# Four changes at once to a one-core transformer block: residual buffers, a load's queue, paired score products and the routing test

## The chip, the cores and the metric

The kernel runs on one core of a Trainium2 chip. The core has five engines with an instruction stream each: TensorE (PE, matrix products into PSUM), VectorE (DVE), ScalarE (ACT), GpSimd (POOL) and SyncE (SP), which here only issues transfers. The engines wait for each other through semaphores. The metric is the device time of one execution in microseconds; lower is better.

## The reference

Input and output are 8 x 1024 rows of 256 numbers, in float32. The block has three parts, each added to its input:

```python
x = x + 0.5 * ffn(layernorm(x))
x = x + attention(layernorm(x))
x = x + 0.5 * ffn(layernorm(x))
```

`attention` is causal, with 16 heads of 16 numbers, a relative position bias from a table, and an output projection `y @ W_proj.T + b_proj`. `ffn` is larger than its name:

```python
y1 = ln(x + mha(x))                 # 4 heads of 64, over the 8 rows of axis 0
gates = softmax(xf @ wg)            # 8 experts
idx = argmax(gates)
mask1 = one_hot(idx, E)
loc = sum((cumsum(mask1, 0) - 1) * mask1, -1)   # place in the expert's line
keep = loc < cap                    # cap = 8192 / 8 = 1024
slot = where(keep, idx * cap + loc, E * cap)
h = einsum('ecd,edf->ecf', disp, w1) + b1       # disp: the kept rows by slot
y = einsum('ecf,efd->ecd', h, w2) + b2
out = where(keep, gate_val * y[slot], 0)
return ln(y1 + out)
```

There is no nonlinearity between the expert's two products, so the kernel multiplies its weights w1 and w2 first and applies one 256 x 256 matrix to each row.

## The kernel before

The rows are cut into 64 tiles of 128 (`TILES`), and four tiles make a group, of which there are 16 (`NG`). The program is fully unrolled: `each(count, body)` calls `body(n, n % 2)`. A stage is a `Phase` with one block of code for each engine, and the order on each engine is the order in which the code is written. A semaphore count that an engine waits for is the only tie between them. The stages are: constants; the first FFN (attention, routing, gather and expert products); the projection to queries, keys and values; the attention core; the output projection; the second FFN in the same code as the first.

**Output projection** (`attention_out`). Per group POOL copies the attention's result into `y` (L2314), PE transposes it (8 records, L2330), ACT and DVE copy the transposed tiles out (L2356, L2374), and PE makes 16 records of products in two halves (L2346). DVE adds the projection's bias to the residual that SP has loaded into `xr` (L2382) and then the product of each half (L2387, twice). ACT's queue stores `xr` (L2364). `xr` has two buffers, and the load of group n waits for the store of group n - 2 (L2304 issues the load).

**Attention core** (`attention_core`). A unit is four heads of one sequence. SP loads for each unit the queries (twelve transfers, L1829), the keys (six, L1833), the transposed near bias `biasT` (eight, L1838) and the near bias (L1847), in this order. PE's first products (L1906) want keys and queries, DVE's first instruction (L2197) the near bias, ACT's first (L2098) `biasT`.

**FFN attention** (`ffn_attention`). PE's order is written out by hand, and a tile's scores (L439) are four products, one for each head: queries of the head pair `qT[:, u, h // 2]` stationary, keys `kT[:, u, h]` moving, 128 columns. `kT` is zero where the other head of the pair lies, so both heads of a pair have the same stationary side. L428 is the product to the values, of 256 columns.

**Routing** (`ffn`). `link` makes DVE wait for its own instruction before the next one. After `attend_vector`, the half's attention code, DVE makes the mask, the places, the slots and the free slots that dropped rows go to, and then eight chunks of one-hot tiles with which PE builds the inverse list (L1269). The part of a chunk that holds the gate values is scaled by ACT (L1132), and for the chunks in `MINE` by DVE (L1420). A dropped row of rank r gets the offset of the interval of free slots [fbeg, fend) in which r lies: `a3` is (r >= fbeg), `b3` is (r < fend) (L1388), their product (L1389) times `off` (L1390) is summed over the experts.

## Time and profile before

| | us |
|---|---|
| Runs of the kernel before | 2779.59, 2789.35, 2786.78 (median 2786.78) |
| Profiled execution, its own time | 2785.7 |
| Its span in the profile | 2784.0 |
| PE busy | 2344.2 (84%) |
| DVE busy | 2148.9 (77%) |
| ACT busy | 1658.3 (60%) |
| POOL busy | 838.5 (30%) |
| FFN attention, first and second half | 19 to 487, 2059 to 2522 |
| Routing, first and second | 487 to 538, 2522 to 2574 |
| Gather and expert products | 538 to 760, 2574 to 2784 |
| Attention core | 981 to 1967 |
| Output projection | 1967 to 2059 |

The stages' bounds are read from the timeline. A row of the trace names the line of the kernel, the engine, the operation, what it writes and reads, its shape and how often it stands there. A time in brackets is how long the engine sat idle before it, and what ended that. "PEld" is the loading of a product's stationary side, which runs beside PE's products. "SPq" and "ACTq" are the transfers that an engine issues.

### The profile page before, as it was taken

What the parts mean: (1) busy time and instruction counts of PE and PEld (TensorE: products, weight loads), DVE (VectorE), ACT (ScalarE), POOL (GpSimd) and SP (SyncE); (2) the same over time, 40 slices, a digit from 0 to 9 for tenths busy, and PEclk for the clock granted to TensorE, in tenths of its full rate; (3) what the DMA queues carried; (4) which work ended last, traced back from release to release, by engine and by line L of the source; (5) the groups of instructions that cost most, each with busy time, mean ns of one, the idle gap of its engine ahead of it and who ended that gap; (6) DMA issues with size and microseconds to landing.
All of it is one profiled execution on the core that took longest, in us unless ns stands there. A gap on an engine that the chain in (4) does not pass through costs nothing. (4 is left out here: it accounts for less than half of the span.)

```text
span 2784.0 us, 46914 instructions
## 1 busy us (share of the span) xinstructions
PE 2344.2 (84%) x15864; PEld 1420.1 (51%) x15864; DVE 2148.9 (77%) x5653; ACT 1658.3 (60%) x3995; POOL 838.5 (30%) x853
## 2 busy tenths in 40 slices
PE   5999998867479959999999999999869999994263
PEld 4666665745345514444444444444646666663243
DVE  5888887727779868889898898987447888877067
ACT  3455453416534439999999999999315455452154
POOL 2343443264634420000000000000123343431746
PEclk8999999879789969999999999999989999996677
DMA  4132214372245464454554554542441121211722
GB/s 121 52 100 72 69 51 140 131 254 102 79 138 169 160 129 98 95 108 99 102 105 94 107 105 93 110 99 45 131 149 54 46 69 46 69 46 46 207 80 76
DMA packets 244687, 281.60 MB, mean 101 GB/s; under 512 B 41808, under 2 KB 212880, under 8 KB 243808
## 3 DMA queue, kind: packets, MB, share of 16 engines
q1 hardware_dynamic: 218192, 218.81, 30.7%
q0 software_dynamic: 16384, 50.35, 5.7%
q10 hardware_dynamic: 9872, 9.45, 1.0%
q8 instruction: 127, 2.08, 0.3%
q14 instruction: 112, 0.92, 0.1%
HBM read 190.63 MB, written 94.16 MB: 102 GB/s over the span
## 5 line engine op out<-in xcount | busy, mean ns | idle before, releaser
L2197 DVE CUSTOM_DVE_ANT_0 banks<-banks,attn_bias 128x128 f32<-128x128 f32 (+7 forms) x1024 | 760.1, 779 | 109.3 <-PE banks L1906 83.2
L2110 ACT ACTIVATE attn_probT<-banks 128x512 f32<-128x512 f32 x1152 | 623.6, 623 | 61.3 <-PE banks L1923 50.7
L1906 PE MATMUL banks<-attn_kst,attn_qst 96*128 96x512 bf16 (+3 forms) x1536 | 421.3, 336 | 23.1 <-DMA attn_kst<-kparts 13.0
L1923 PE MATMUL banks<-attn_qst,attn_kst 99*128 99x256 bf16 (+3 forms) x2176 | 411.6, 281 | 14.7 <-ACT attn_probT L2110 7.1
L1945 PE MATMUL banks<-attn_probT,attn_vb 128*32 128x256 f32 (+3 forms) x4352 | 316.2, 400 | 7.8 <-ACT attn_probT L2110 7.4
L1923 PEld LDWEIGHTS banks<-attn_qst,attn_kst 99*128 99x128 bf16 x2176 | 187.2, 97 | 169.6 <-ACT attn_probT L2110 55.5
L2255 POOL CAST attn_lowp<-attn_lowT 128x32 bf16<-128x32 f32 x64 | 13.5, 211 | 851.3 <-DVE attn_lowT L2205 851.3
L410 PE MATMUL banks<-ffn_xT,winT 128*128 128x512 f32 x512 | 250.9, 613 | 6.0 <-ACT ffn_w L610 2.9
L1906 PEld LDWEIGHTS banks<-attn_kst,attn_qst 96*128 96x128 bf16 x1536 | 117.4, 97 | 256.0 <-DVE attn_low L2197 158.5
L2098 ACT COPY banks<-attn_biasT 128x512 f32<-128x512 f32 x384 | 228.4, 630 | 28.5 <-DMA attn_biasT<-neardT 21.8
L870 POOL TENSOR_TENSOR ffn_xs<-ffn_xs,row_ffn_out 128x1024 f32<-128x1024 f32 x32 | 75.4, 2356 | 416.3 <-DVE ffn_xs L752 390.2
L580 ACT ACTIVATE ffn_xs<-banks,ffn_xs 128x128 f32<-128x128 f32 x512 | 182.9, 380 | 13.1 <-DVE ffn_xs L717 11.5
L1945 PEld LDWEIGHTS banks<-attn_probT,attn_vb 128*32 128x32 f32 x4352 | 106.4, 109 | 133.4 <-ACT attn_probT L2110 70.0
L619 ACT COPY ffn_xs<-banks 128x256 f32<-128x256 f32 x128 | 48.3, 377 | 203.5 <-PE banks L459 200.2
L1083 POOL DMA_INDIRECT ffn_xs<-rows,ffn_inv x128 | 123.1, 962 | 148.5 <-DVE ffn_inv L1424 94.5
L1318 PE MATMUL banks<-ffn_w,ffn_xT 128*128 128x256 f32 x512 | 130.4, 408 | 44.0 <-issue 31.4
L610 ACT ACTIVATE ffn_w<-banks,ffn_qk_b 64x512 f32<-64x512 f32 x128 | 87.4, 683 | 128.0 <-PE banks L410 127.2
L717 DVE TENSOR_REDUCE ffn_xs<-banks 128x4 f32<-128x512 f32 x128 | 88.5, 692 | 92.3 <-PE banks L439 92.1
L439 PEld LDWEIGHTS banks<-ffn_w,ffn_xs 128*128 128x128 f32 x1024 | 135.6, 200 | 23.7 <-issue 20.3
L439 PE MATMUL banks<-ffn_w,ffn_xs 128*128 128x128 f32 x1024 | 145.3, 287 | 0.8 <-DVE ffn_xs L739 0.8
L2197 DVE DVE_READ_ACCUMULATOR2_ANT attn_low<- 128x1 f32 x1024 | 144.9, 141 | 0.1
L725 DVE TENSOR_SCALAR ffn_xs<-ffn_xs 128x128 f32<-128x128 f32 x512 | 137.5, 331 | 4.5
(254 smaller groups left out, 4500.2 us busy)
## 6 DMA issues: line engine op xcount, KB each, us to landing
rows<-ffn_xs SPq DMA_DIRECT2D x64, 512.0 KB, 3.1
attn_qst<-qparts SPq DMA_DIRECT2D x384, 64.0 KB, 2.8
attn_kst<-kparts SPq DMA_DIRECT2D x192, 128.0 KB, 4.9
ffn_xs<-in_L_ffn_w_dram SPq DMA_DIRECT2D x16, 1024.0 KB
attn_biasT<-neardT SPq DMA_DIRECT2D x128, 128.0 KB, 4.9
attn_bias<-neard SPq DMA_DIRECT2D x128, 128.0 KB, 2.2
qparts<-qkv_part SPq DMA_DIRECT2D x32, 384.0 KB, 2.8
kparts<-qkv_part SPq DMA_DIRECT2D x32, 384.0 KB, 2.8
```

The source lines that it names most:

```text
L410: mm = nc.tensor.matmul(bank[QK], core.winT[:, k, j * P:(j + 1) * P], xT[:, u, k, :], start=(k == 0), stop=(k == KB - 1))
L439: mm = nc.tensor.matmul(bank[SC[t % 2]][:, h * P:(h + 1) * P], qT[:, u, h // 2, t * P:(t + 1) * P], kT[:, u, h, t * P:(t + 1) * P], start= ...
L580: ins = nc.scalar.activation(prob[:, t % 2, h, :], bank[SC[t % 2]][:, h * P:(h + 1) * P], ACT.Exp, bias=negm[:, t % 2, h:h + 1], scale=1.0 ...
L725: ins = nc.vector.tensor_scalar(prob[:, t % 2, h, :], prob[:, t % 2, h, :], rinv[:, t % 2, h:h + 1], None, ALU.mult)
L1083: pool.indirect_dma_start(xs[:, n, t, :], None, rows, bass.IndirectOffsetOnAxis(ap=inv[:, i:i + 1], axis=0)).then_inc(s_got[n % 2], 16)
L1318: mm = nc.tensor.matmul(part, xT[:, u, k, t * P:(t + 1) * P], w12[:, k, expert(n, u)], start=False, stop=(k == KB - 1), skip_group_check=True)
L1906: mm = nc.tensor.matmul(score[k % 2][:, a:e], qst[0:K6, u, half, hh, ii * P:(ii + 1) * P], kst[0:K6, u, hh, a:e], start=True, stop=True)
L1923: mm = nc.tensor.matmul(tbank[t % 3][:, at:at + nb * P], kst[:, u, hh, j * P:(j + 1) * P], qst[:, u, half, hh, x:x + nb * P], start=(k == ...
L1945: mm = nc.tensor.matmul(obank[32 * hh:32 * hh + 32, x:x + nb * P], vb[:, u, j, hh, :], probT[:, g % 2, i, at:at + nb * P], start=hh not in ...
L2098: nc.scalar.copy(tbank[t % 3].rearrange("p (a c) -> p a c", a=2), over(near[:, 0:2 * P], 2, 1)).then_inc(s_seed, 1)
L2110: nc.scalar.activation(probT[:, g % 2, i, 0:w], tbank[t % 3][:, 0:w], ACT.Exp, scale=-1.0).then_inc(s_exp, 1)
L2197: nc.vector.tensor_tensor_reduce(out=part, in0=part, in1=bias[:, hh, T - w:T], scale=1.0, scalar=BIG, op0=ALU.add, op1=ALU.min, accum_out= ...
```

## The change

Four places are edited. (1) In the output projection `xr` gets four buffers (`XR = 4`), each with its own load and store semaphores, so the load of group n waits for the store of group n - 4. (2) In the attention core the six key loads of the first unit are issued by ACT, ahead of all its work, and no longer by SP; those of later units stay on SP. (3) In FFN attention one product makes two heads' scores: the moving side is 256 columns, two products a tile. (4) In routing the interval test becomes a sum of steps: with `step` the difference of neighbouring offsets, the sum over e of (r >= fbeg[e]) * step[e] is the offset of the last interval that begins at or below r. Two 512-column operations go and two small ones come. Five small operations move from the routing chain to the start of the FFN phase, and `MINE` is (3, 7) in place of (2, 5).

```diff
@@ -435,10 +435,10 @@
...
             if not (under(n, 1) and t < 2):
                 pe.wait_ge(s_seed, 4 * n + t - 1)
-            for h in range(FH):
-                mm = nc.tensor.matmul(bank[SC[t % 2]][:, h * P:(h + 1) * P], qT[:, u, h // 2, t * P:(t + 1) * P],
-                                      kT[:, u, h, t * P:(t + 1) * P], start=False, stop=(h == FH - 1),
-                                      skip_group_check=True)
+            for j in range(FH // 2):
+                mm = nc.tensor.matmul(bank[SC[t % 2]][:, 2 * j * P:(2 * j + 2) * P].rearrange("p (h c) -> p h c", h=2),
+                                      qT[:, u, j, t * P:(t + 1) * P], kT[:, u, 2 * j:2 * j + 2, t * P:(t + 1) * P],
+                                      start=False, stop=(j == FH // 2 - 1), skip_group_check=True)
             mm.then_inc(s_sps, 1)
 
...
@@ -936,7 +936,7 @@
...
     FB = FF // P
     CT = TILES // NG * 2
-    MINE = (2, 5)
+    MINE = (3, 7)
     with Phase(core, name) as ph:
         logits = ph.sb("logits", [P, TILES, NE])
...
@@ -957,12 +957,12 @@
...
         onb, ona = lent(0, CHUNKS, CT, P), lent(4, CHUNKS, CT, 2 * TILES)
         dif, ex, cand = (lent(8 + i / 4, TILES, NE) for i in range(3))
-        hot, scan, a3, b3 = (lent(9 + i / 4, NE, TILES) for i in range(4))
+        hot, scan, a3 = (lent(9 + i / 4, NE, TILES) for i in range(3))
         w1 = [lent(10 + i, KB, FF) for i in range(2)]
         w2 = [lent(12 + i, FB, C) for i in range(4)]
         onest = tile("onest", TILES)
-        eidx, ebase, tot, cnt, free, fend, fbeg, off = (tile(n, NE) for n in (
-            "eidx", "ebase", "tot", "cnt", "free", "fend", "fbeg", "off"))
+        eidx, ebase, tot, cnt, free, fend, fbeg, off, step = (tile(n, NE) for n in (
+            "eidx", "ebase", "tot", "cnt", "free", "fend", "fbeg", "off", "step"))
         ei = tile("ei", NE, dt=I32)
         rowtot = tile("rowtot", NE + 1)
...
@@ -1337,16 +1337,19 @@
...
                 dve.wait_ge(s_dve, n[0])
 
-            attend_vector(dve)
-            over_yet(dve)
             V = nc.vector
-            link(V.tensor_reduce(mx[:, :], logits[:, :, :], AX.X, ALU.max))
-            V.tensor_tensor(dif[:, :, :], logits[:, :, :], over(mx[:, :], NE, 2), ALU.subtract).then_inc(s_dif, 1)
             dve.wait_ge(s_iota, 1)
             link(V.tensor_copy(eidx[:, :], ei[:, :]))
             link(V.tensor_scalar(ebase[:, :], eidx[:, :], float(CAP), None, ALU.mult))
             link(V.memset(onest[:, :], 1.0))
-
+            dve.wait_ge(s_ib, 1)
+            link(V.tensor_copy(ib_f[:, :], ib[:, :]))
+            dve.wait_ge(s_ni, 1)
+            link(V.tensor_copy(number[:, :], ni[:, :]))
+            attend_vector(dve)
+            over_yet(dve)
+            link(V.tensor_reduce(mx[:, :], logits[:, :, :], AX.X, ALU.max))
+            V.tensor_tensor(dif[:, :, :], logits[:, :, :], over(mx[:, :], NE, 2), ALU.subtract).then_inc(s_dif, 1)
             dve.wait_ge(s_dif, 1)
             link(V.tensor_scalar(cand[:, :, :], dif[:, :, :], 0.0, -float(NE), ALU.is_ge, ALU.mult))
...
@@ -1376,6 +1379,8 @@
...
             link(V.tensor_tensor(off[:, :], ebase[:, :], cnt[:, :], ALU.add))
             link(V.tensor_tensor(off[:, :], off[:, :], fbeg[:, :], ALU.subtract))
+            V.tensor_copy(step[:, 0:1], off[:, 0:1])
+            link(V.tensor_tensor(step[:, 1:NE], off[:, 1:NE], off[:, 0:NE - 1], ALU.subtract))
 
             dve.wait_ge(s_ex, 1)
...
@@ -1385,9 +1390,7 @@
...
             link(V.tensor_scalar(rank[:, :], dscan[:, :], base[:, NE:NE + 1], -1.0, ALU.add, ALU.add))
             link(V.tensor_tensor(a3[:, :, :], over(rank[:, :], NE, 1), over(fbeg[:, :], TILES, 2), ALU.is_ge))
-            link(V.tensor_tensor(b3[:, :, :], over(rank[:, :], NE, 1), over(fend[:, :], TILES, 2), ALU.is_lt))
-            link(V.tensor_tensor(a3[:, :, :], a3[:, :, :], b3[:, :, :], ALU.mult))
-            link(V.tensor_tensor(a3[:, :, :], a3[:, :, :], over(off[:, :], TILES, 2), ALU.mult))
+            link(V.tensor_tensor(a3[:, :, :], a3[:, :, :], over(step[:, :], TILES, 2), ALU.mult))
             link(V.tensor_reduce(t2[:, :], a3[:, :, :].rearrange("p e t -> p t e"), AX.X, ALU.add))
             link(V.tensor_tensor(t2[:, :], t2[:, :], rank[:, :], ALU.add))
...
@@ -1400,10 +1403,6 @@
...
             link(V.tensor_copy(bf[:, :], bcol[:, :]))
             link(V.tensor_copy(af[:, :], acol[:, :]))
-            dve.wait_ge(s_ib, 1)
-            link(V.tensor_copy(ib_f[:, :], ib[:, :]))
-            dve.wait_ge(s_ni, 1)
-            link(V.tensor_copy(number[:, :], ni[:, :]))
             for u in range(2):
                 stored(dve, u)
...
@@ -1817,6 +1816,12 @@
...
             return isinstance(n, int) and n == NU - 1
 
+        def load_keys(queue, n, u):
+            for r, a in enumerate(K_PARTS):
+                queue.dma_start(kst[r * AD:(r + 1) * AD, u, :, :],
+                                kd[bass.ds(n * HG * AD, HG * AD), a, :].rearrange("(h d) t -> d h t", d=AD)
+                                ).then_inc(s_load[u], 16)
+
         block = ph.block()
 
...
@@ -1829,10 +1834,8 @@
...
                                      qd[bass.ds(n * HG * AD, HG * AD), a, half * HW:(half + 1) * HW].rearrange(
                                          "(h d) t -> d h t", d=AD)).then_inc(s_load[u], 16)
-                for r, a in enumerate(K_PARTS):
-                    sp.dma_start(kst[r * AD:(r + 1) * AD, u, :, :],
-                                 kd[bass.ds(n * HG * AD, HG * AD), a, :].rearrange("(h d) t -> d h t", d=AD)
-                                 ).then_inc(s_load[u], 16)
+                if not under(n, 1):
+                    load_keys(sp, n, u)
                 for hh in range(HG):
                     for at, w in ((0, 2 * P), (2 * P, P)):
...
@@ -2087,6 +2090,8 @@
...
         @block.scalar
         def _(act):
+            load_keys(act, 0, 0)
+
             def seed(n, u, t):
                 pieces = TILE[t][4]
...
@@ -2284,13 +2289,14 @@
...
 
     nc = core.nc
+    XR = 4
     rows, outs = (a.rearrange("(g t p) c -> g p t c", p=P, t=GT) for a in (x, out))
     with Phase(core, "proj") as ph:
         y = ph.sb("y", [P, 2, GT, C])
         yT = ph.sb("yT", [P, 2, KB, GW])
-        xr = ph.sb("xr", [P, 2, GT, C])
-        s_load = [ph.sem("load0"), ph.sem("load1")]
-        s_store = [ph.sem("store0"), ph.sem("store1")]
+        xr = ph.sb("xr", [P, XR, GT, C])
+        s_load = [ph.sem(f"load{i}") for i in range(XR)]
+        s_store = [ph.sem(f"store{i}") for i in range(XR)]
         s_y, s_xb, s_tps, s_tsb0, s_tsb1, s_ops, s_osb = (ph.sem(x) for x in (
             "y", "xb", "tps", "tsb0", "tsb1", "ops", "osb"))
...
@@ -2299,10 +2305,11 @@
...
         def _(sp):
             def body(n, u):
-                if not under(n, 2):
-                    sp.wait_ge(s_store[u], (n - u) * 8)
-                sp.dma_start(xr[:, u, :, :], rows[bass.ds(n, 1), :, :, :].rearrange(
-                    "o p t c -> p (o t) c")).then_inc(s_load[u], 16)
+                v, turns = n % XR, n // XR
+                if turns:
+                    sp.wait_ge(s_store[v], 16 * turns)
+                sp.dma_start(xr[:, v, :, :], rows[bass.ds(n, 1), :, :, :].rearrange(
+                    "o p t c -> p (o t) c")).then_inc(s_load[v], 16)
             each(NG, body)
 
...
@@ -2362,10 +2369,10 @@
...
                 act.wait_ge(s_osb, 2 * n + 2)
                 act.dma_start(outs[bass.ds(n, 1), :, :, :].rearrange("o p t c -> p (o t) c"),
-                              xr[:, u, :, :]).then_inc(s_store[u], 16)
+                              xr[:, n % XR, :, :]).then_inc(s_store[n % XR], 16)
             each(NG, body)
-            for u in range(2):
-                act.wait_ge(s_store[u], 16 * (NG // 2))
+            for v in range(XR):
+                act.wait_ge(s_store[v], 16 * (NG // XR))
 
         @block.vector
...
@@ -2378,15 +2385,16 @@
...
                 if not (isinstance(n, int) and n == NG - 1):
                     yT_out(n + 1, 1 - u)
-                dve.wait_ge(s_load[u], (n - u) * 8 + 16)
-                nc.vector.tensor_tensor(xr[:, u, :, :], xr[:, u, :, :], over(core.rows["proj"][:, :], GT, 1),
+                v = n % XR
+                dve.wait_ge(s_load[v], 16 * (n // XR + 1))
+                nc.vector.tensor_tensor(xr[:, v, :, :], xr[:, v, :, :], over(core.rows["proj"][:, :], GT, 1),
                                         ALU.add).then_inc(s_xb, 1)
                 dve.wait_ge(s_xb, n + 1)
                 for h in range(2):
                     dve.wait_ge(s_ops, 2 * n + h + 1)
-                    nc.vector.tensor_tensor(xr[:, u, 2 * h:2 * h + 2, :],
+                    nc.vector.tensor_tensor(xr[:, v, 2 * h:2 * h + 2, :],
                                             bank[4 + h].rearrange("p (t c) -> p t c", t=2),
-                                            xr[:, u, 2 * h:2 * h + 2, :], ALU.add).then_inc(s_osb, 1)
+                                            xr[:, v, 2 * h:2 * h + 2, :], ALU.add).then_inc(s_osb, 1)
             each(NG, body)
 
...
```

How the instructions move is seen in the order on three engines. On PE, in the first FFN's attention, a stretch before and in the change (`ffn_w` and `ffn_xs` are the memory that `qT` and `kT` lie in):

```order
 L410 MATMUL banks<-ffn_xT,winT 128x512 x6
 L393 MATMUL banks<-ident,ffn_xs 128x128 x4
-L439 MATMUL banks<-ffn_w,ffn_xs 128x128 x8
-L393 MATMUL banks<-ident,ffn_xs 128x128 x4
-L428 MATMUL banks<-winT,ffn_xT 128x256 x4
-L439 MATMUL banks<-ffn_w,ffn_xs 128x128 x4
...
+L439 MATMUL banks<-ffn_w,ffn_xs 128x256 x4
+L393 MATMUL banks<-ident,ffn_xs 128x128 x4
+L428 MATMUL banks<-winT,ffn_xT 128x256 x4
+L439 MATMUL banks<-ffn_w,ffn_xs 128x256 x2
```

The four products of a tile have become two of twice the width, at the same place between the same neighbours. In the trace each of these float32 products is two records, so a tile has eight records of 128 columns before.

On SP, at the start of the attention core, before:

```order
L1829 DMA attn_qst<-qparts 16x4x512 x12
L1833 DMA attn_kst<-kparts 16x4x1024 x6
L1838 DMA attn_biasT<-neardT 128x256
...
L1847 DMA attn_bias<-neard 128x256 x4
L1829 DMA attn_qst<-qparts 16x4x512 x12
```

and the same place in the change, where L1834 is the query load, L1841 `biasT`, L1850 the near bias and L1821 the keys of the second unit:

```order
L1834 DMA attn_qst<-qparts 16x4x512 x12
L1841 DMA attn_biasT<-neardT 128x256
...
L1850 DMA attn_bias<-neard 128x256 x4
L1834 DMA attn_qst<-qparts 16x4x512 x12
L1821 DMA attn_kst<-kparts 16x4x1024 x6
```

The first unit's keys are gone from between the queries and the tables; they stand at the head of ACT's stream, before its first copy from `biasT`.

On DVE, at the start of each FFN phase (here the first):

```order
 L159 UNCONDITIONAL_BRANCH
 L1331 UNCONDITIONAL_BRANCH
+L1342 CAST ffn_eidx<-ffn_ei 128x8
+L1343 TENSOR_SCALAR ffn_ebase<-ffn_eidx 128x8
+L1344 MEMSET ffn_onest 128x64
+L1346 CAST ffn_ibf<-ffn_ib 128x128
+L1348 CAST ffn_number<-ffn_ni 128x64
 L791 MEMSET ffn_w 128x4096
 L767 MEMSET gatew 128x128
```

Five small operations, which stood in the routing chain as L1346 to L1348, L1404 and L1406, stand ahead of the memset that opens the phase.

## Rows read from the trace of the kernel before

**Rows 1.** Groups by line, 1960 to 2059 (busy us, mean ns, idle before).

```profile
L2346 PE MATMUL banks<-wprojT,proj_yT 128*128 128x256 f32 x256 | 60.4, 390 | 11.3 <-DVE proj_xr L2387 11.3
...
L2382 DVE TENSOR_TENSOR proj_xr<-proj_xr,row_proj 128x1024 f32<-128x1024 f32 x16 | 20.5, 1282 | 31.8 <-DMA proj_xr<-x 31.8
```

**Rows 2.** Waits of SP's queue, 1965 to 2062 (total us, times, longest).

```profile
SPq L2304 <- DMA x<-proj_xr: 75.9, 14, 9.5
```

**Rows 3.** Timeline of the output projection (start, us, instruction, idle before).

```profile
1974.82 3.62 PE L2346 MATMUL banks<-wprojT,proj_yT 128*128 128x256 f32 x16
...
1978.47 0.69 DVE L2387 TENSOR_TENSOR proj_xr<-banks,proj_xr 128x512 f32<-128x512 f32 x1 [0.59 <-PE banks L2346]
...
1979.15 3.62 PE L2346 MATMUL banks<-wprojT,proj_yT 128*128 128x256 f32 x16
...
2049.80 3.69 PE L2346 MATMUL banks<-wprojT,proj_yT 128*128 128x256 f32 x16 [1.61 <-DVE proj_xr L2387]
...
2054.37 1.29 DVE L2387 TENSOR_TENSOR proj_xr<-banks,proj_xr 128x512 f32<-128x512 f32 x2
```

**Rows 4.** Windows (engines' busy us, PEclk, DMA share, GB/s).

```profile
1990.00:2010.00 20.00, 17.39 (x94) 14.75 (x92) 9.52 (x13) 2.35 (x4) 3.43 (x4) 1.00 0.63 202
995.00:1000.00 5.00, 1.58 (x5) 0.45 (x5) 1.54 (x7) 2.23 (x4) 0.01 (x1) 0.50 1.14 286
```

**Rows 5.** DMA issues, 1950 to 2060 (KB each, us to landing).

```profile
proj_xr<-x SPq DMA_DIRECT2D x16, 512.0 KB, 3.9
```

**Rows 6.** Timeline at the start of the attention core.

```profile
987.17 2.77 SPq L1833 DMA_DIRECT2D attn_kst<-kparts  x6
...
993.77 1.85 SPq L1847 DMA_DIRECT2D attn_bias<-neard  x4
...
995.43 0.48 PE L1906 MATMUL banks<-attn_kst,attn_qst 96*128 96x128 bf16 x2 [12.98 <-DMA attn_kst<-kparts]
...
998.25 0.30 DVE L2197 CUSTOM_DVE_ANT_0 banks<-banks,attn_bias 128x128 f32<-128x128 f32 x1 [13.87 <-DMA attn_bias<-neard]
```

**Rows 7.** Timeline of the second routing.

```profile
2524.18 2.67 POOL L863 TENSOR_TENSOR ffn_xs<-ffn_xs,row_ln_b 128x1024 f32<-128x1024 f32 x1
2524.57 2.31 DVE L1346 CAST ffn_eidx<-ffn_ei 128x8 f32<-128x8 int32 x1
...
2541.10 0.69 DVE L1388 TENSOR_TENSOR ffn_xs<-ffn_rank,ffn_fend 128x512 f32<-128x512 f32 x1
...
2546.77 0.23 DVE L1404 CAST ffn_ibf<-ffn_ib 128x128 f32<-128x128 int32 x1
```

**Rows 8.** Timeline at the end of the second routing.

```profile
2568.12 2.02 PE L1269 MATMUL banks<-ffn_xs 128*128 128x128 f32 x16 [1.28 <-ACT ffn_xs L1132]
...
2570.77 2.02 PE L1269 MATMUL banks<-ffn_xs 128*128 128x128 f32 x16 [0.63 <-ACT ffn_xs L1132]
```

**Rows 9.** Timeline where the two FFN halves start.

```profile
23.59 2.34 POOL L877 TENSOR_TENSOR ffn_xs<-ffn_xs,row_ln_b 128x1024 f32<-128x1024 f32 x1 [3.67 <-DMA ffn_xs<-in_L_attn_x_dram]
...
23.88 2.08 DVE L769 TENSOR_TENSOR fourth<-ident 128x16 f32<-128x16 f32 x1
...
2060.01 3.47 DVE L791 MEMSET ffn_w<- 128x4096 f32 x1 [4.35 <-PEq L2288]
...
2063.39 1.34 DVE L677 BATCH_NORM_STATS2 ffn_xs<-ffn_xs 128x6 f32<-128x256 f32 x4
```

**Rows 10.** Timeline: scores beside another product, and a slowed score block.

```profile
2134.01 1.92 PE L439 MATMUL banks<-ffn_w,ffn_xs 128*128 128x128 f32 x8
...
2192.70 1.89 PE L428 MATMUL banks<-winT,ffn_xT 128*128 128x256 f32 x8
...
2194.42 1.05 PE L439 MATMUL banks<-ffn_w,ffn_xs 128*128 128x128 f32 x8
...
2195.32 0.60 PE L449 MATMUL banks<-ident,ffn_xs 128*128 128x128 f32 x4
```

**Rows 11.** Timeline during the second gather.

```profile
2623.09 1.97 PE L1223 MATMUL banks<-ident,ffn_y 128*128 128x128 f32 x8 [23.40 <-issue]
```

## The prediction

> **What bounds the kernel now.** The page's busy shares come first: PE is busy 84% of the span, DVE 77%, ACT 60%, so no stage is short of work and each edit has to be read in its own stage. Then the trace, stage by stage.
>
> In the output projection (1967 to 2059) the groups by line show PE's product L2346 idle for 11.3 us on DVE's additions, and DVE's L2382 idle for 31.8 us on the load of the residual [rows 1]. SP's queue, which issues that load, stands for 75.9 us in 14 waits for the store out of the same buffer [rows 2]. Sixteen groups go through two buffers, so 14 loads wait for a store: this stage is bound by the round "add, store, load, add", not by an engine. The timeline shows the pace without the wait: the second and third product begin at 1974.82 and 1979.15, 4.33 us apart, while the last begins at 2049.80 [rows 3], which is (2049.80 - 1979.15)/13 = 5.43 us a group on average.
>
> At the start of the attention core nothing but transfers goes on. SP issues the six key loads from 987.17 for 2.77 us, then the tables, the last of them from 993.77; PE begins at 995.43 with the keys, DVE at 998.25 with the near bias [rows 6].
>
> In routing DVE runs one chain, each instruction waiting for the last, and PE and ACT follow; in FFN attention PE is nearly always busy, and the scores are a part of its own row of work.
>
> **Output projection, two more buffers.** What a buffer's turn must hold can be read off the pace. L2382 starts about 0.8 us after its group's product and the second L2387 ends 4.34 us after it (1978.47 + 0.69 - 1974.82 [rows 3]), so at 5.43 us a group two buffers leave 2 x 5.43 - 3.54 = 7.3 us for the store and the load after it; that is just what the pair takes, which agrees with a landing of 3.9 us for a load [rows 5] and about as much for a store. Four buffers at 4.33 us leave 4 x 4.33 - 3.54 = 13.8 us. The pair could take almost twice its time before DVE waits again. So I expect SP's waits to end unnoticed and every group at 4.33. What is late next is PE itself: 16 products and 8 transposes fill the 4.33 (3.62 of it in L2346 [rows 3]), and DVE has about 3.2 us of work in a group. The last product then begins at 1974.82 + 13 x 4.33 + 3.46 = 2034.57 (the last group has no transposes ahead of it: 16 records at 0.2155 us), the last addition ends 4.34 later at 2038.91, and before it ended at 2054.37 + 1.29 = 2055.66 [rows 3]. That is **-16.7 us**. Nothing excludes a part of it: the 1.05 MB of a group in 4.33 us is 242 GB/s, and this stage moved 202 GB/s [rows 4]. That the engines can carry more is seen at the start of the core, with 286 GB/s [rows 4]. I take -16.7; the bounds are 0 and -16.8.
>
> **Core start, keys on ACT's queue.** SP's table loads move forward by the 2.77 us that the keys' six issues took [rows 6]. ACT has nothing to do then: its first work waits for biasT, issued after the keys. The order on ACT is six issues and then that work, so nothing is held up. DVE's start at 998.25 is the end of a load issued from 993.77, 4.5 us before, so it can come to about 995.5, and PE's 995.43 goes earlier too. The other end is 0: in 995 to 1000 the transfers filled the DMA engines (share 1.14 [rows 4]), so earlier issue may only mean a longer queue. Bounds -2.8 and 0; I take the issue, since DVE's start lies 4.5 us behind the first issue of its load, close to the 3.9 us that a load takes elsewhere [rows 5]. **-2.5 us**.
>
> **Routing.** Gone from the chain of the second half: L1388 and its product L1389, 0.73 us each from start to start (0.69 long [rows 7]), against two step operations of 1 and 7 columns, which I put at 0.14 each (an estimate: less than the 0.23 of L1404): -1.17. The moved L1404 and its like L1406 took from 2546.77 to 2547.26: -0.49 [rows 7]. The other three moved ones look dearer than they are. L1346 took 2.31 us for 8 columns, and it ends at 2526.88, when POOL's L863 does (2524.18 + 2.67 = 2526.85) [rows 7]: it was held by POOL, and the next instruction on DVE, the 512-column L1351, is of the kind that I expect to be held in its place. So I take from these three only what lay behind POOL's end, about 0.45 us, where the upper end is 2.31 and some 0.4 for the two short ones, 2.7.
>
> The Trainium skill bears on this (SBUF — State Buffer, section "SBUF: two separate sides"): DVE and GpSimd share a port pair as an exclusive lock, and the loser stands for the whole instruction. The row agrees to 0.03 us. By that rule the gain is the 0.45, without it 2.7.
>
> At the end of routing PE waits for ACT's scaling before each of its last two blocks, 0.63 us each, and starts them 2.65 us apart [rows 8]; 16 records at 0.1115 are 1.78. With chunk 7 scaled on DVE the last one follows at once: -0.86. Together -3.0 in the second half. The five moved operations stand there at the head of DVE's line, ahead of the memset L791 that starts at 2060.01 and directly behind which L677 begins the chain of the half [rows 9]: five of them at L1404's 0.23 or a little less, +1.1. Net **-1.9 us**. In the first half DVE has slack at the start: L769 took 2.08 us for 16 columns, again held by POOL [rows 9], so the 1.1 disappears; without that cover it would cost 1.1. At the end of that routing ACT, busy with weight copies, sets the time, so the shorter DVE chain brings nothing and only the last block counts: **-0.9 us** (range 0 to -3).
>
> **Scores.** A tile's scores are 8 records of 128 columns at 0.1115 us each, 0.89 us; the block of L439 starts 0.90 us before what follows it. L428 runs 8 records of 256 columns in 2194.42 - 2192.70 = 1.72 us [rows 10], so four take 0.86. The stationary side is loaded half as often, but these loads lie beside matmuls now. So 0.03 us a tile; 64 tiles in each of two halves stand on PE's own line: 128 x 0.03 = **-3.5 us**. Other blocks of L439 take 0.99 from start to start; if two heads a product removed the 0.1 as well, it is 128 x 0.11 = -14. The low end is -3 or, were the two-head form to read its operand slower, 0. I take the small value, since the 0.1 stands at a block's edge, which stays.
>
> **Clock.** In 8 of 28 iterations of FFN attention the granted clock fell and a score block took 1.92 us in place of 1.05 (eight rows like the one at 2134.01 [rows 10]), with some 1.55 us lost in the iteration. The blocks are rearranged in time, so this number can be 3 or 14 after: -8 to +9 us, taken as 0.
>
> **Sum.** -16.7 - 2.5 - 1.9 - 0.9 - 3.5 = -25.5. The profiled execution took 2785.7 us (span 2784.0); the median of the runs, 2786.8, is 1.1 above. 2785.7 - 25.5 = 2760.2, and on the median's footing 2761.
>
> **The rivals.**
> *The forecast*, four buffers free the projection and the small ones add: 2761. Chance 0.77.
> *Transfers hold the projection.* If 202 GB/s were the limit, 1.05 MB takes 5.2 us, a gain of 14 x 0.26 = 3.6 in place of 16.7: 2761 + 13 = 2774. For it: the rate would have to rise by a fifth, with reads and writes mixed. Against it: the 286 GB/s, and that SP idled 75.9 us, so the present rate is made by the wait. Chance 0.11, half of it still faster by over 0.3%.
> *Scores save the block's edge too*: -14 in place of -3.5, 2750. Chance 0.07.
> *Slower: a longer starvation in the gather.* In the second FFN's expert stage PE stood 23.40 us with nothing to wait for that the profile shows [rows 11], while GpSimd gathered rows by DMA; it is likely the loading of PE's instructions behind those transfers. The change takes 1,024 records off PE ahead of it, so the point in the code at which this happens can shift. One more such stand in each half: +46.8, 2761 + 46.8 = 2808. It decides from 25.5 + 8.4 = 34 us, so one alone (2784) is no change. Against it: the stages behind attention are the same, instruction for instruction. Chance 0.05.
>
> The Trainium skill says of this (Runtime: NRT & Kernel Launch, section "Instruction fetch mechanics") that the engine fetches ahead in 16 KiB blocks and the cost is mostly hidden. By that rule this rival is nothing; the row of 23.40 us speaks against it.
>
> **How the numbers follow.** What a measurement can tell from no change is 0.3%, 8.4 us: from 2778.4 to 2795.2. Low end: scores at -14 and two or three dips fewer give 2746, so 2745. High end: the transfer-bound projection, 2774, and a few us of spread in the runs (2779.6 to 2789.4 before), 2777. Faster takes the forecast, the scores and half of the transfer case, 0.77 + 0.07 + 0.05 = 0.89, less 0.01 for mishaps; same is the rest of the transfer case and a single stand, 0.07; slower 0.05.
>
> **What would show it.** In the profile after: no or short waits of L2382 for its load, L2346 groups 4.33 apart, the stage some 17 us shorter; DVE's first L2197 some 2.5 us nearer to the start of the core; the 512-column instruction after the routing's subtraction taking about 2.3 in place of 0.43; L439 with 512 records of 256 columns at 0.2155. I am wrong if L2382's wait goes over to the load's landing (DMA share near full and groups over 5 us), if the gather's stands grow, or if L439's block costs over 0.9.

## The result and the profile after

The changed kernel takes 2763.36 us (median of four runs, 2759.59 to 2764.06), the kernel before 2786.66 (four runs). The ratio is 0.9912, 95% interval 0.9900 to 0.9924: 23.3 us faster, where 25.5 were forecast, inside the range of 2745 to 2777. The profiled execution of the changed kernel is its shortest run, 2759.59 us.

The head of its page (span; busy us, share, instructions):

```profile
span 2757.9 us, 45893 instructions
...
PE 2334.6 (85%) x15352; PEld 1387.7 (50%) x15352; DVE 2151.4 (78%) x5653; ACT 1657.1 (60%) x3995; POOL 838.6 (30%) x853
```

PE has 512 product records fewer and 9.6 us less of busy time. Each stage begins at an instruction that both traces have, so their stages can be laid side by side ("memset" is DVE's L791, which opens an FFN):

| stage (us) | before | after | difference | forecast |
|---|---|---|---|---|
| Constants | 19.43 | 20.66 | +1.2 | 0 |
| FFN 1, start to memset | 0.92 | 2.15 | +1.2 | hidden |
| FFN 1, attention | 466.73 | 465.29 | -1.4 | -1.75 |
| FFN 1, routing | 50.64 | 49.97 | -0.7 | -0.9 |
| FFN 1, gather and experts | 230.39 | 225.62 | -4.8 | 0 |
| Projection to queries, keys, values | 212.86 | 212.34 | -0.5 | 0 |
| Core, SP's first load to DVE's first L2197 (L2202 after) | 17.28 | 16.65 | -0.6 | -2.5 |
| Core, the rest | 969.11 | 968.24 | -0.9 | 0 |
| Output projection | 91.74 | 76.12 | -15.6 | -16.7 |
| FFN 2, start to memset | 0.91 | 2.15 | +1.2 | +1.1 |
| FFN 2, attention | 462.23 | 459.50 | -2.7 | -1.75 |
| FFN 2, routing | 50.59 | 47.32 | -3.3 | -3.0 |
| FFN 2, gather and experts | 211.17 | 211.89 | +0.7 | 0 |

**Output projection.** The groups by line, which answer to [rows 1] (product and bias addition are now L2353 and L2390):

```profile
L2353 PE MATMUL banks<-wprojT,proj_yT 128*128 128x256 f32 x256 | 57.7, 379 | 0.0
...
L2390 DVE TENSOR_TENSOR proj_xr<-proj_xr,row_proj 128x1024 f32<-128x1024 f32 x16 | 23.6, 1474 | 0.0
```

Both idle times have gone from 11.3 and 31.8 us to 0.0. SP's queue, the line that answers to [rows 2], still waits, 55.8 us in 12 waits where it was 75.9 us in 14, and the longest is the same:

```profile
SPq L2311 <- DMA x<-proj_xr: 55.8, 12, 9.5
```

This wait is now harmless: the loads run ahead of their use, so SP waits early for a buffer that nobody misses yet, and DVE's L2390 never stands for its load. The engine that uses the data has to be read, not the queue. The timeline (compare [rows 3]):

```profile
1962.01 3.31 PE L2337 MATMUL banks<-ident,proj_y 128*128 128x128 f32 x16 [2.13 <-POOL proj_y L2321]
...
1965.15 3.62 PE L2353 MATMUL banks<-wprojT,proj_yT 128*128 128x256 f32 x16
...
1969.48 3.62 PE L2353 MATMUL banks<-wprojT,proj_yT 128*128 128x256 f32 x16
...
2025.76 7.07 PE L2353 MATMUL banks<-wprojT,proj_yT 128*128 128x256 f32 x32
...
2032.87 0.69 DVE L2395 TENSOR_TENSOR proj_xr<-banks,proj_xr 128x512 f32<-128x512 f32 x1 [0.91 <-PE banks L2353]
```

The products stand 4.33 us apart (1969.48 - 1965.15), and from 1965.15 to 2025.76 there are 14 such steps, 60.61 us: none is stretched. The missing 1.1 us lies ahead of them. PE's first two sets of transposes took 3.31 us for 16 records, where they took 2.08 before. The granted clock fell to 0.50, the lower of its two levels (1.2 GHz), while PE stood idle for 2.13 us ahead of them, and rose to 1.00 (2.4 GHz) at 1964.8, while PE was busy. In the kernel before, PE came out of the same wait (2.14 us) at a granted clock of 1.00. So this is not of the change: among the profiles of the experiments the fall at the stage's start comes and goes, and E7, with the same four buffers at a clock of 1.00, takes 75.01 us for the stage.

**Core start**, to be held against [rows 6]:

```profile
976.04 2.75 ACTq L1821 DMA_DIRECT2D attn_kst<-kparts  x6
...
985.81 2.28 SPq L1850 DMA_DIRECT2D attn_bias<-neard  x4
...
989.86 0.48 PE L1909 MATMUL banks<-attn_kst,attn_qst 96*128 96x128 bf16 x2 [12.35 <-DMA attn_qst<-qparts]
...
992.68 0.30 DVE L2202 CUSTOM_DVE_ANT_0 banks<-banks,attn_bias 128x128 f32<-128x128 f32 x1 [13.24 <-DMA attn_bias<-neard]
```

The keys are issued at the stage's start by ACT, and the last table 9.78 us after it (985.81 - 976.03), where it was 12.80. But DVE starts 6.87 us behind that issue, where it was 4.48. Of the 3.0 us saved in issuing 2.4 went into the time from issue to DVE's start.

**Routing.** The 512-column instruction behind the second routing's subtraction (compare [rows 7]):

```profile
2500.61 2.67 POOL L863 TENSOR_TENSOR ffn_xs<-ffn_xs,row_ln_b 128x1024 f32<-128x1024 f32 x1
...
2501.12 2.45 DVE L1354 TENSOR_SCALAR ffn_xs<-ffn_xs 128x512 f32<-128x512 f32 x1
```

It ends 0.29 us behind GpSimd's instruction and takes 2.45 us, where the same operation stood at 0.43 before: it took the place of the 8-column one, as forecast. The end of the second routing, which answers to [rows 8]:

```profile
2539.51 2.02 PE L1269 MATMUL banks<-ffn_xs 128*128 128x128 f32 x16 [0.63 <-ACT ffn_xs L1132]
...
2542.16 3.81 PE L1269 MATMUL banks<-ffn_xs 128*128 128x128 f32 x32 [0.62 <-ACT ffn_xs L1132]
```

The last two blocks run as one piece of 32 records with one wait ahead of them. And the start of the second FFN (compare [rows 9]):

```profile
2037.20 0.18 DVE L1342 CAST ffn_eidx<-ffn_ei 128x8 f32<-128x8 int32 x1 [3.64 <-POOL ffn_ei L1072]
...
2038.08 0.20 DVE L1348 CAST ffn_number<-ffn_ni 128x64 f32<-128x64 int32 x1
2039.19 3.47 DVE L791 MEMSET ffn_w<- 128x4096 f32 x1 [0.92 <-DVE ffn_number L1348]
```

**Scores.** The score products in the groups by line:

```profile
L439 PE MATMUL banks<-ffn_w,ffn_xs 128*128 128x256 f32 x512 | 141.1, 400 | 0.8 <-DVE ffn_xs L739 0.8
```

512 records of 256 columns in place of 1,024 of 128. The starvation in the gather that a rival was built on, [rows 11], is still there, of the same length and at the same product:

```profile
2596.17 1.97 PE L1223 MATMUL banks<-ident,ffn_y 128*128 128x128 f32 x8 [23.40 <-issue]
```

### The profile page after: what moved, and what is told of

Its sections match the earlier page's. It is cut to its first block and busy times, and to the rows that moved or that the text cites. A ratio compares the mean times of both kernels' runs of the same rounds, so it can differ in the third digit from the quotient of the medians.

```text
span 2757.9 us, 45893 instructions
## 1 busy us (share of the span) xinstructions
PE 2334.6 (85%) x15352; PEld 1387.7 (50%) x15352; DVE 2151.4 (78%) x5653; ACT 1657.1 (60%) x3995; POOL 838.6 (30%) x853
## 5 line engine op out<-in xcount | busy, mean ns | idle before, releaser
L2202 DVE CUSTOM_DVE_ANT_0 banks<-banks,attn_bias 128x128 f32<-128x128 f32 (+7 forms) x1024 | 759.7, 778 | 108.1 <-PE banks L1909 82.8
L2260 POOL CAST attn_lowp<-attn_lowT 128x32 bf16<-128x32 f32 x64 | 13.4, 209 | 850.3 <-DVE attn_lowT L2210 850.3
L410 PE MATMUL banks<-ffn_xT,winT 128*128 128x512 f32 x512 | 250.7, 612 | 6.5 <-ACT ffn_w L610 2.9
L1318 PE MATMUL banks<-ffn_w,ffn_xT 128*128 128x256 f32 x512 | 130.3, 408 | 43.0 <-issue 30.7
L2202 DVE DVE_READ_ACCUMULATOR2_ANT attn_low<- 128x1 f32 x1024 | 143.8, 140 | 0.1
L439 PE MATMUL banks<-ffn_w,ffn_xs 128*128 128x256 f32 x512 | 141.1, 400 | 0.8 <-DVE ffn_xs L739 0.8
L410 PEld LDWEIGHTS banks<-ffn_xT,winT 128*128 128x128 f32 x512 | 90.3, 192 | 93.3 <-issue 73.8
```

Of the source, the lines that this page charges most:

```text
L410: mm = nc.tensor.matmul(bank[QK], core.winT[:, k, j * P:(j + 1) * P], xT[:, u, k, :], start=(k == 0), stop=(k == KB - 1))
L439: mm = nc.tensor.matmul(bank[SC[t % 2]][:, 2 * j * P:(2 * j + 2) * P].rearrange("p (h c) -> p h c", h=2), qT[:, u, j, t * P:(t + 1) * P], ...
L1318: mm = nc.tensor.matmul(part, xT[:, u, k, t * P:(t + 1) * P], w12[:, k, expert(n, u)], start=False, stop=(k == KB - 1), skip_group_check=True)
L2202: nc.vector.tensor_tensor_reduce(out=part, in0=part, in1=bias[:, hh, T - w:T], scale=1.0, scalar=BIG, op0=ALU.add, op1=ALU.min, accum_out= ...
```

## The experiments

They ran on two chips, E1 to E4 on the one that their results number 4 and E5 to E12 on number 8; the result of the first comparison names no chip. The kernel before takes 2716.57 us on chip 4 and 2715.1 to 2715.5 on chip 8, 70 less than in the first comparison (this is looked at in the last section). Each ratio is to runs of the kernel before on the same chip. The stages of the kernel before are from its own profile, E11, on chip 8. E3, E7, E8 and E9 ran once each and are read by their stages alone.

**E1, four buffers alone.** The edit to `attention_out` (`XR = 4` and its semaphores), nothing else.

> The kernel before with four residual buffers in the output projection and nothing else. Theory (the buffer round was the bound): the stage shortens by 15 to 16 us and the whole by the same, ratio about 0.9943; no wait of DVE's bias addition for its load. Rival (part of it is a phase between this stage and the others, or a given-back wait later): the stage shortens by 15 but the whole by less than 10.

2697.04 us against 2716.57, ratio 0.9927 (0.9910 to 0.9944): 19.5 us. The stage takes 76.45 us, 15.4 less than the 91.81 of E11. On E1's own chip the stage with two buffers takes 92.80 (E2), 95.54 (E3) and 92.94 us (E4). All four of these profiles have the fall of the clock at the stage's start, E3's the longest; against E2 and E4 the gain is 16.4 to 16.5. The buffer round is shown as the cause of the main gain; nothing was given back later. The interval of the whole, 15 to 24 us, holds all these figures.

**E5, three buffers.**

```diff
-    XR = 4
+    XR = 3
...
-                act.wait_ge(s_store[v], 16 * (NG // XR))
+                act.wait_ge(s_store[v], 16 * len(range(v, NG, XR)))
```

> The kernel before with three residual buffers. Theory (a buffer's round needs 7.3 us, three buffers at 4.33 us a group leave 9.45): the same gain as with four, 15 to 16 us in the stage. Rival (store and load take longer when they overlap more): only a part, 5 to 12 us, with waits of DVE's bias addition left.

2697.65 us, ratio 0.9935 (0.9919 to 0.9952), stage 74.93. Its groups by line:

```profile
L2348 PE MATMUL banks<-wprojT,proj_yT 128*128 128x256 f32 x256 | 57.8, 379 | 0.0
...
L2385 DVE TENSOR_TENSOR proj_xr<-proj_xr,row_proj 128x1024 f32<-128x1024 f32 x16 | 23.9, 1494 | 0.0
```

No idle time either. Three buffers do it, as the account of 9.45 against 7.3 us said; the fourth brings nothing measurable. The fair partner of this stage is E7's 75.01 with four buffers, since both have a granted clock of 1.00 at the stage's start; E12's 76.11 and E1's 76.45 have the fall.

**E2, the scores alone.**

> The kernel before with two heads per score product and nothing else. Theory (the saving of 0.12 us in an iteration of FFN attention is given back where DVE's L690 meets GpSimd's L858, which lasts 2.60 in place of 2.45 us): iterations of 26.72 and 26.87 us side by side, the whole unchanged within 2 us, ratio 0.999 to 1.001. Rival (as predicted, 0.03 us a tile): all iterations at 26.68, the whole 3.5 us shorter, ratio 0.9987. The number of clock dips may move it by 1.55 us each.

2714.9 us, ratio 0.9997 (0.9987 to 1.0007). The theory fell. It came from the trace of the changed kernel, in which iterations of 26.72 and 26.87 us (from one L495 to the next) alternate, where the kernel before has 26.80 only; the longer ones are those in which GpSimd's L858 lasts longer, with DVE's L690 held beside it. Both kinds in the changed kernel:

```profile
2107.86 2.45 POOL L858 TENSOR_TENSOR ffn_xs<-ffn_xs,row_ln_g 128x1024 f32<-128x1024 f32 x1 [1.72 <-DVE ffn_xs L711]
...
2134.57 2.60 POOL L858 TENSOR_TENSOR ffn_xs<-ffn_xs,row_ln_g 128x1024 f32<-128x1024 f32 x1 [1.73 <-DVE ffn_xs L711]
```

But E1, E3 and E4, which have the old scores, show 26.80 and 26.95 side by side, E5 and E11, with the old scores too, nearly only 26.80, and E12 and E7, with the new ones, only 26.72. So the 0.15 us of GpSimd comes with either kernel, and at each of its two levels the edit saves 0.08 us an iteration: 0.02 us a tile, not 0.03. The level goes with the chip more than with the edits: of the 32 instructions of L858 21 to 24 last 2.60 us or more in the four profiles of chip 4, and 0 to 4 in the eight of chip 8. Of four score blocks in an iteration three keep about 0.03 us each (0.96 from start to start in E12, 0.99 in E11); the first gives it up before PE's next product of L410 begins. For 128 tiles that is 2.6 us, which the interval of E2 (-3.5 to +1.9 us) neither excludes nor shows; the saving rests on the iterations.

**E3, the keys on ACT's queue alone.**

> The kernel before with the first unit's keys loaded from ACT's queue and nothing else. Theory (the transfers' bytes set the start): DVE's first instruction in the core comes 0.6 us nearer to the stage's start than in the kernel before (17.28 us). Rival (the issue sets it): 2.5 us nearer.

DVE starts 16.84 us after the stage's start, in E11 17.04. E1, E2, E4, E5 and E11, with the keys on SP, have 16.83 to 17.05; E3, E7, E8 and E12, with the keys on ACT, 16.13 to 16.84. The queue is worth 0 to 0.9 us, not 2.5.

**E6, near bias first.** In the changed kernel, for the first unit:

```diff
+                if under(n, 1):
+                    near(0)
                 for hh in range(HG):
                     for at, w in ((0, 2 * P), (2 * P, P)):
                         sp.dma_start(biasT[:, u, hh, at:at + w],
...
             load(0, 0)
-            near(0)
             load(1, 1)
```

> The changed kernel with the near bias of the first unit loaded before its transposed near bias. Theory (DVE's first instruction waits for the last of the first unit's bytes): DVE starts the core 1.5 to 3 us earlier, just behind PE's first product, and the whole gains that much, unless ACT, whose table now lands later, takes it back: then 0. Rival (all is landed at one time whatever the order): no change at all in DVE's start, 16.6 us from the stage's start.

**E9, the same with the keys back on SP.**

> The changed kernel with the near bias before its transposed form, and the first unit's keys back on SP's queue. Theory (what DVE's start waits for is the last byte ahead of it, so the order matters and the queue that issues hardly): DVE starts 14.3 to 14.6 us after the stage's start, against 14.0 with the keys on ACT, 16.6 to 16.9 with the near bias last. Rival (both edits are needed): 16 us or more.

E6: 13.99 us from the stage's start. E9: 14.61. Against the same queue in the old order (16.13 to 16.84, and 16.83 to 17.05) the order of the loads is worth 2.1 to 2.9 us at DVE's start; E6 against E9 gives the queue 0.6. Near bias and DVE's start in E9 and, below, in E10, which has E6's core:

```profile
957.41 1.85 SPq L1851 DMA_DIRECT2D attn_bias<-neard  x4
...
963.21 0.30 DVE L2200 CUSTOM_DVE_ANT_0 banks<-banks,attn_bias 128x128 f32<-128x128 f32 x1 [11.21 <-PE banks L1909]
```

```profile
952.41 1.85 SPq L1852 DMA_DIRECT2D attn_bias<-neard  x4
...
960.13 0.50 PE L1910 MATMUL banks<-attn_kst,attn_qst 96*128 96x128 bf16 x2 [11.95 <-POOL attn_kst L2275]
...
960.60 0.30 DVE L2203 CUSTOM_DVE_ANT_0 banks<-banks,attn_bias 128x128 f32<-128x128 f32 x1 [10.49 <-PE banks L1910]
```

DVE now waits for PE's first product and no longer for a load. In E10 the stage starts at 946.70, and PE waits for GpSimd's memset of the key rows, which ends 13.4 us after the stage's start in every profile, and not for a transfer. In E6 and E9 PE still waits for its transfers, and starts 0.1 and 0.7 us later than in E10. So memset and transfers are late next, close together. ACT, which waits for `biasT`, starts 1.6 us later than with the old order (E6 17.80 us from the stage's start, E8 16.19) and in E9 3.3 later (19.86, against 16.54 in E11), and that takes part of the gain back: from the stage's start to the output projection E6 takes 982.71 us, E10 983.44, E9 984.20, E12 984.43, E8 984.86, E11 986.04. E6 as a whole: 2690.82 us, ratio 0.9907 (0.9890 to 0.9923), which can't be told from E12's.

**E4, the routing edits alone.**

> The kernel before with the routing edits (step test, five operations moved, chunks 3 and 7 on DVE) and nothing else. Theory: in both halves together 2.5 to 3 us (routing -0.7 and -3.3, starts about +1.2 in the second), ratio 0.999. Rival: the 4.8 us that the first expert stage lost between the profiles of before and after come from here, since this stage follows the routing directly: 7 us or more, ratio 0.9975.

2712.72 us, ratio 0.9984 (0.9975 to 0.9994). Routing 49.97 and 47.33 us, in E11 50.63 and 50.59; starts +1.25 each. The first expert stage takes 197.51 us, in E11 197.53: the 4.8 us that this stage lost in the first comparison do not come from these edits. The stage goes from 194.5 to 197.7 us over the twelve profiles of the experiments, with no tie to any edit.

**E7, the five operations back in the routing chain.**

```diff
-            link(V.tensor_copy(ib_f[:, :], ib[:, :]))
-            dve.wait_ge(s_ni, 1)
-            link(V.tensor_copy(number[:, :], ni[:, :]))
             attend_vector(dve)
...
             link(V.tensor_copy(af[:, :], acol[:, :]))
+            dve.wait_ge(s_ib, 1)
+            link(V.tensor_copy(ib_f[:, :], ib[:, :]))
```

> The changed kernel with the five small operations back in the routing chain. Theory: the start of the second FFN gets 1.2 us shorter, its routing only 0.9 to 1.1 longer, since the first of them stands in for an operation that GpSimd holds anyway; net 0 for the kernel. In that routing L1346's like takes 2.3 us again. Rival (they are worth their move): routing 2.5 us or more longer.

The second routing takes 48.42 us, with the operations moved 47.33: 1.09 longer. The start takes 0.90 against 2.16: 1.26 shorter. So their move is worth nothing in the second half, and the first routing changes by 0.2 us (50.16).

**E8, chunks 2 and 5 on DVE again.**

> The changed kernel with chunks 2 and 5 on DVE in place of 3 and 7. Theory: the last inverse block waits for ACT again, the gates are ready 0.8 us later in the second routing and 0.6 to 0.9 in the first. Rival: ACT ends at the same time, no difference over 0.2 us.

Second routing 48.29 us, 0.96 longer than with (3, 7), as expected. First routing 48.50 us, **shorter** by 1.5 than the changed kernel's 49.97. Both expectations missed this. The other profiles with (3, 7) and the moved operations have 49.60 to 49.97, E10 with (2, 5) has 48.77, so the difference is 0.8 to 1.5 us. The end of the first routing in the changed kernel, and in E8:

```profile
523.35 10.73 ACT L1132 ACTIVATE ffn_xs<-ffn_xs,ffn_zero,ffn_gate 128x64 f32<-128x64 f32 x32
...
534.22 3.81 PE L1269 MATMUL banks<-ffn_xs 128*128 128x128 f32 x32 [0.57 <-ACT ffn_xs L1132]
```

```profile
522.69 14.46 PE L1269 MATMUL banks<-ffn_xs 128*128 128x128 f32 x128
...
523.53 5.42 ACT L1132 ACTIVATE ffn_xs<-ffn_xs,ffn_zero,ffn_gate 128x64 f32<-128x64 f32 x16
...
529.42 5.41 ACT L1132 ACTIVATE ffn_xs<-ffn_xs,ffn_zero,ffn_gate 128x64 f32<-128x64 f32 x16 [0.47 <-DVE ffn_xs L1415]
```

In the first half ACT is at copies of expert weights and transposed tiles until about 523.5 and only then scales its four remaining chunks. With (3, 7) these are 2, 4, 5 and 6, back to back to 534.08, and PE stands 0.57 us for chunk 6 and has two blocks to do behind it. With (2, 5) PE finds chunk 2 ready from DVE, never waits again (128 records in one piece of 14.46 us), and ACT waits for DVE for only 0.47 us; in the kernel before ACT waited 2.27 us there. PE is then the bound.

**E12, the changed kernel there.**

> The changed kernel, unchanged, on the chip of the experiments. Theory: 22 to 25 us under the kernel before there too, ratio about 0.991; output projection 15 to 16 us shorter, first routing 0.7 and second 3.3 shorter, second FFN start 1.2 longer, core start 0 to 0.6 shorter, an iteration of FFN attention 0.08 shorter at equal state of GpSimd. Rival: the 4.8 us that the first expert stage lost in the first comparison belong to the change and are seen again.

2693.29 us against 2715.10, ratio 0.9916 (0.9903 to 0.9930). Projection 76.11 us (E11 91.81), routing 49.97 and 47.33, second start 2.16, core start 16.13. First expert stage 195.55, second 173.24 (E11 197.53, 173.83).

**E10, near bias first and the chunks by half.** E6's edit and

```diff
-    MINE = (3, 7)
+    MINE = (2, 5) if turn == 0 else (3, 7)
```

> The changed kernel with the near bias loaded first and with chunks 2 and 5 on DVE in the first half, 3 and 7 in the second. Theory: the first routing 1.1 to 1.5 us shorter than in the changed kernel, the second as in it, the core's start 2.8 us shorter; together 4 us under the changed kernel, ratio to the kernel before about 0.9895. Rival: the differences of single stages drown in the clock's dips (1.55 us each) and the median is the changed kernel's within 1.5 us.

2688.26 us, ratio 0.9893 (0.9878 to 0.9908): 5.0 us under E12 by the medians; the two intervals overlap, so that one is faster than the other is not shown by the whole times. The stages show what they should: first routing 48.77 (49.97), second 47.32, core start 13.90 (16.13), together 3.4 us. It has the lowest median of all versions; E6's interval overlaps with it.

## Why the prediction came true, step by step

**Output projection.** Right in mechanism, and in size where the clock is the same: 15.6 us in the two profiles, of which the fall of the clock at the stage's start took 1.1 back. Pairs that both have it give 16.4 to 16.8 (E2 and E4 against E1 and E12), and E7, like the first profile of before without it at the start, gives 16.7 (91.74 against 75.01). Every profile with two buffers has a further fall later in the stage; in the kernel before it comes at 67.5 us from the stage's start, and DVE's additions L2382 stand 5.10 and 5.24 us apart there, less than the mean of 5.43, so it is not part of the gain. The groups run at the 4.33 us that two unstalled groups of the old trace showed. In the transfer rival's sum 14 x 0.26 should be 14 x 0.24, 3.4 us for 3.6, which changes nothing. The rival of transfers as the limit is out: the same bytes went at 246 GB/s in the stage's later part (2005 to 2025), where 202 had been the rate made by the wait.

**Core start.** The step "SP's table loads move forward by the 2.77 us that the keys' six issues took" was right for the issues and wrong for the landing. 3 us earlier issue gave 0.6. I had put both ends down and taken the wrong one: a landing 4.5 us behind the first issue looked like a landing of 3.9 elsewhere, but the share of 1.14 in [rows 4] said that the DMA engines were full. What counts is what stands ahead of the load waited for: with the near bias ahead of the 1 MB of `biasT` DVE's start came 2.1 us or more earlier on either queue (E6, E9). The step that failed is the whole 2.77 us taken as gain; the range had the other end, 0, and the truth lies near it.

**Second routing.** Right in each term: the chunks 0.96 (E8; forecast 0.86), the five operations 1.09 (E7; 0.49 + 0.45), and the step test, which had no run of its own, by difference the rest of the 3.27, 1.2 (1.17). The 512-column operation was held in place of the 8-column one. As the Trainium skill has it (SBUF — State Buffer, section "SBUF: two separate sides"), the loser of the shared port pair waits for the whole instruction, and the 2.45 us agree with that. The cost at the start was +1.24 (forecast 1.1).

**First routing.** The number, -0.7 for -0.9, is near for a wrong reason. The step that failed is "ACT, busy with weight copies, sets the time, so the shorter DVE chain brings nothing and only the last block counts". E8 shows the shorter DVE chain alone worth 2.1 us there (50.63 to 48.50), since ACT had waited 2.27 us for DVE, and that the new chunks cost 0.8 to 1.5 of it. That the two nearly met the forecast was luck.

**Scores.** The term was mis-sized: 0.02 us a tile and not 0.03, since one block in four saves nothing. 2.6 us by the iterations, in place of 3.5. The 0.1 at a block's edge stays, so the rival of -14 is out.

**Clock.** 8 slowed iterations before, 7 after, 1.55 us each: -1.6 in the profile, well inside the -8 to +9 that were set aside for it. In such an iteration PE comes out of two waits for DVE (0.65 and 1.0 us), and while the score block behind them runs the granted clock is 0.50; the iterations at a clock of 1.00 have the same waits. In the experiments the counts run from 5 (E1, E3) to 10 (E6, E9, E10), for the kernel before 9 (E11) and the changed one 7 (E12). They are noise of up to 8 us between executions, not part of the change as far as 14 profiles show.

**The sum.** Projection -15.6, second routing and start -2.0, first routing -0.7, core start -0.6, scores -2.6 are -21.5, against 23.3 by the medians of the first comparison and 21.8 on chip 8; the clock's dips, 1.55 us each, are enough for the difference. The first half's start, +1.2, is rightly not in it: start and attention without thirteen iterations in the middle take 112.4 us in E4, 112.7 to 113.2 in the other experiments with the moved operations, and 112.8 to 113.1 in those without. The two profiles differ by 26.1 us in their own times (2785.7 and 2759.59), near the 25.5 partly by luck: the core's start and the scores brought 2.8 us less than forecast, and the first expert stage brought 4.8 that stand in no term. The 4.8 us of the first expert stage are not in the change: E4 and E12 have 197.5 and 195.6 there, E11 197.5.

**Gather.** The slower rival did not come about: the stand was 23.40 us in both traces.

## What to carry to other kernels

Before a buffer is added, work out what a buffer's round must hold (count times pace, less the time in use) and compare it with the round observed: here it said that three would do and what the pace would then be. When several loads are waited for at a stage's start and the DMA engines are full, put the one that is waited for first in front; another queue for issuing is worth little. A choice of which engine does which chunk is right for one neighbour only: the same `(3, 7)` gained 1.0 us where ACT was free and lost 0.8 to 1.5 where it was busy.

## What had not been expected

The same kernel took 2787 us in the first comparison and 2715 to 2717 on both chips of the experiments. The stages of the kernel before, in the first profile and in E11: first expert stage 230.39 and 197.53 us, second 211.17 and 173.83, every other stage behind the constants the same within 0.3 us. The second gather and expert stage in the first profile, by line, and below it the same in E11:

```profile
L1318 PE MATMUL banks<-ffn_w,ffn_xT 128*128 128x256 f32 x256 | 68.0, 417 | 36.4 <-issue 30.4 <-ACT banks L1155 5.8
...
L1223 PE MATMUL banks<-ident,ffn_y 128*128 128x128 f32 x128 | 20.9, 316 | 51.2 <-issue 26.4 <-ACT ffn_y L1142 24.8
```

```profile
L1318 PE MATMUL banks<-ffn_w,ffn_xT 128*128 128x256 f32 x256 | 64.9, 411 | 7.3 <-ACT banks L1155 7.3
...
L1223 PE MATMUL banks<-ident,ffn_y 128*128 128x128 f32 x128 | 19.1, 297 | 23.8 <-ACT ffn_y L1142 23.8
```

In the first profile PE stood 30.4 and 26.4 us with nothing that the profile names; in E11 not at all. A part of the stand of 23.40 us [rows 11] can be followed further. In the middle of it DVE and ACT wait too:

```profile
2618.93 0.88 DVE L1461 SCALAR_TENSOR_TENSOR ffn_xs<-banks,ffn_gnow,ffn_xs 128x256 f32<-128x256 f32 x2 [19.10 <-remote]
...
2622.01 1.03 ACT L1142 COPY ffn_y<-ffn_xs 128x1024 f32<-128x1024 f32 x1
```

L1461 waits for PE's product of L1318. The trace puts the last record of that product at 2599.31, but DVE goes on only at 2618.93 ("remote" says that the profile finds no instruction to which the signal belongs). From there DVE, ACT and PE's L1223 at 2623.09 follow in 4.2 us. So 19 of the 23.4 us lie ahead of the product's signal, and the rest is the chain behind it. The Trainium skill (Runtime: NRT & Kernel Launch, section "Instruction fetch mechanics") says that crossing from one 16 KiB block of instructions to the next is mostly hidden. E11 agrees with that. The first profile would not, if loading is what these stands are, and this is not shown: from 2599.7 to 2623.0 its DMA table has 1,482 packets of the gathers' queue and none of an instruction queue. The cause is open. No run here separates the chip from what else was going on beside it. Why GpSimd's L858 lasts 2.45 or 2.60 us is open as well.
